# Conv1 outputs, phase differences and conv2 operands stored position by position, graphs innermost

## What is computed

```python
h = jnp.maximum(_layernorm(x, axis=-1), 0.0)            # (64, 128 nodes, 128)
xc = jnp.transpose(h, (0, 2, 1))
c = jax.nn.relu(_bn(_conv1d(xc, conv1_w, 0), ...))      # 1 tap
c = _bn(_conv1d(c, conv2_w, 8), ...)                    # 17 taps, padding 8
x_conv = jnp.transpose(jax.nn.relu(c + xc), (0, 2, 1))
A = jnp.exp(-dist(h @ w_se.T)) * adj                    # dist: squared distances
x_nmp = A @ jax.nn.relu(h @ w_msg.T + b_msg)
gi, gh = concat([x_conv, x_nmp]) @ w_ih.T + b_ih, h @ w_hh.T + b_hh
x = x + gru(gi, gh, h)                                  # gates r, z, n
x = x + adj @ (relu(layernorm(x)) @ weight) + bias      # second layer
```

## Time and profile before

| | |
|---|---|
| median of 3 runs | 414.94 us (414.62 to 416.28) |
| the profiled execution | 415.42 us, its span 413.2 us |
| PE busy | 352.8 us, 85% of the span |
| DVE, ACT, POOL busy | 289.6, 206.6, 175.7 us |
| mean granted TensorE clock | 0.924 of full speed |
| time from one conv1(a) to the next, steps 2 to 6 | 44.5 us each |

### The profile page before, as it was taken

One profiled execution on the slowest core, in us unless ns is written; L12 is line 12 of the kernel. 1 busy time (PEld: TensorE's weight loads), 2 busy tenths in 40 slices (PEclk: granted clock), 3 DMA queues, 4 the chain that ended last, 5 costly groups with the idle time before them and its releaser, 6 DMA issues.

```text
span 413.2 us, 6302 instructions
## 1 busy us (share of the span) xinstructions
PE 352.8 (85%) x2196; PEld 322.7 (78%) x2196; DVE 289.6 (70%) x736; ACT 206.6 (50%) x402; POOL 175.7 (43%) x140
## 2 busy tenths in 40 slices
PE   6465765997999799979999799979997999989935
PEld 6465755876898689869998799878986899889825
DVE  4768687757787679757875888767985787662471
ACT  2144841554634674475736573567437663442332
POOL 7524264020593039601872069203960197035021
PEclk9688888996999899998999899989999899999975
DMA  7500010000030003100210013000100000001001
GB/s 266 218 0 2 0 52 27 0 2 1 28 106 22 0 4 101 52 0 2 89 66 1 2 35 119 1 2 16 62 26 1 2 27 26 2 0 52 0 0 51
DMA packets 7806, 15.08 MB, mean 37 GB/s; under 512 B 992, under 2 KB 1376, under 8 KB 7648
## 3 DMA queue, kind: packets, MB, share of 16 engines
q1 hardware_dynamic: 7488, 14.56, 10.1%
q10 hardware_dynamic: 288, 0.14, 0.1%
HBM read 10.50 MB, written 4.19 MB: 36 GB/s over the span
## 4 chain that ended last, share of the span: by engine, by line
issue 43%; POOL 32%; DVE 11%; PE 7%; ACT 4%; DMA 1%; POOLq 0%; ACTq 0%; DVEq 0%
POOL work L1107 4%; POOL rs L1066 4%; POOL rs L1061 4%; POOL base L1117 3%; POOL base L1123 3%; POOL base L1119 3%; POOL px L769 3%; POOL px L759 3%; POOL ac L765 2%; POOL px L767 2%; POOL px L762 2%; DVE hn L802 2%; ACT hn L548 1%; DVE cx_lo L858 1%; PE pP L283 1%
## 5 line engine op out<-in xcount | busy, mean ns | idle before, releaser
L1066 POOL TENSOR_TENSOR rs<-ve,neg_half 128x4 f32<-128x4 f32 x16 | 16.1, 1008 | 150.5 <-DVE ve L899 150.5
L262 PE MATMUL pP<-cx_hi,conv_hi 128*128 128x256 f32 x176 | 55.6, 316 | 3.5 <-DVE conv_lo L863 3.5
L263 PE MATMUL pP<-cx_lo,conv_hi 128*128 128x256 f32 x176 | 52.6, 299 | 0.0
L264 PE MATMUL pP<-cx_hi,conv_lo 128*128 128x256 f32 x176 | 52.4, 298 | 0.0
L262 PE MATMUL pQ<-cx_hi,conv_hi 128*128 128x256 f32 x144 | 45.6, 317 | 3.0 <-DVE conv_lo L863 3.0
L263 PE MATMUL pQ<-cx_lo,conv_hi 128*128 128x256 f32 x144 | 43.0, 299 | 0.0
L264 PE MATMUL pQ<-cx_hi,conv_lo 128*128 128x256 f32 x144 | 43.0, 299 | 0.0
L262 PEld LDWEIGHTS pP<-cx_hi,conv_hi 128*128 128x128 f32 x176 | 35.4, 201 | 3.7 <-DVE conv_lo L863 3.7
L1061 POOL TENSOR_TENSOR rs<-ve,neg_half 128x8 f32<-128x8 f32 (+1 forms) x9 | 17.1, 1902 | 44.9 <-DVE ve L789 43.6
L263 PEld LDWEIGHTS pP<-cx_lo,conv_hi 128*128 128x128 f32 x176 | 35.2, 200 | 0.0
L264 PEld LDWEIGHTS pP<-cx_hi,conv_lo 128*128 128x128 f32 x176 | 35.0, 199 | 0.0
(11 more groups left out here) (233 smaller groups left out, 1044.3 us busy)
## 6 DMA issues: line engine op xcount, KB each, us to landing
x_ring<-x_in SPq DMA_DIRECT2D x16, 256.0 KB, 2.6
adj_ring<-adj_in SPq DMA_DIRECT2D x16, 256.0 KB, 3.4
out<-x_ring SPq DMA_DIRECT2D x16, 256.0 KB, 2.0
work<-conv_in SPq DMA_DIRECT2D x1, 1088.0 KB, 7.2
x_ring<-gate_in SPq DMA_DIRECT2D x1, 576.0 KB, 7.7
work<-bias_in SPq DMA_DIRECT2D x1, 132.0 KB, 7.1
early<-early_in SPq DMA_DIRECT2D x1, 129.5 KB, 3.0
late<-late_in ACTq DMA_DIRECT2D x1, 128.0 KB, 3.2
```

What stands on the lines that cost most here:

```text
L262: pe.matmul(acc, w_hi, m_hi, start=start, stop=False)
L263: pe.matmul(acc, w_hi, m_lo, start=False, stop=False)
L264: return pe.matmul(acc, w_lo, m_hi, start=False, stop=stop)
L1066: pool.tensor_tensor(rs2[g % 2][:], ve2[g % 2][:], neg_half[:, 0:GG], ALU.pow).then_inc(rs2_set, 1)
```

## The change

The axes "graph" and "position" are exchanged in `c1`, `ac`, `px`, `cx_hi`, `cx_lo` and `base`: a tile that was [phase, 8 graphs, 36 positions] is now [phase, 36 positions, 8 graphs]. The PSUM halves of conv2 and s22, s12, s32 have their columns in the same new order. `xc_hi` and `xc_lo` stay graph by graph, with the two phases of one e side by side within a graph (64 words), since the gates want graphs outermost. It follows for the accesses:

- The data operand of each of the 960 conv2 matmuls was eight runs of 32 words, 36 words apart, starting at word j; it is one run of 256 words, starting at word 8j.
- `conv1_out` on ACT wrote 16 runs of 32 words; it now writes 512 single words, 8 words (32 bytes) apart.
- `conv_round` on ACT read 512 adjacent words of `base`; it now reads single words 8 words apart, and writes adjacent ones. `conv_lo_out` on DVE does the same with one of its two inputs.
- `own` on POOL read hT in runs of 32 words; it now reads single words 128 words apart.
- `pre` 2 and 5 on POOL had 16 runs of 35 words, now two of 280. The other operations of POOL, `split_hi`, `split_lo`, `between` and `conv_out` cover the same adjacent words as before.
- `gates_c` read runs of 32 adjacent words, now of 64.

Each engine has the same instructions in the same order, with the same waits: 1620 rows on PE, 501 on DVE, 301 on ACT, 133 on POOL, 42 on SP. Lines of the changed kernel are 3 higher than before from `by_graph` to `conv_lo_out`, then 2 higher.

```diff
-        c1 = sb("c1", [128, PH, CG, QP])
-        ac = sb("ac", [128, 2, CG, QP])
-        px = sb("px", [128, 8, CG, QP])
-        cx_hi = sb("cx_hi", [128, 9, CG, QP], F32R)
-        cx_lo = sb("cx_lo", [128, 9, CG, QP], F32R)
+        c1 = sb("c1", [128, PH, QP, CG])
+        ac = sb("ac", [128, 2, QP, CG])
+        px = sb("px", [128, 8, QP, CG])
+        cx_hi = sb("cx_hi", [128, 9, QP, CG], F32R)
+        cx_lo = sb("cx_lo", [128, 9, QP, CG], F32R)
...
-        base = [sb(f"base{i}", [128, 2, CG, QN]) for i in range(2)]
-        xc_hi = sb("xc_hi", [128, PH, CG, QN], F32R)
-        xc_lo = sb("xc_lo", [128, PH, CG, QN], F32R)
+        base = [sb(f"base{i}", [128, 2, QN, CG]) for i in range(2)]
+        xc_hi = sb("xc_hi", [128, 2, CG, 2 * QN], F32R)
+        xc_lo = sb("xc_lo", [128, 2, CG, 2 * QN], F32R)
...
+        def by_graph(e):
+            return base[e][:].rearrange("p s m g -> p g (s m)")
...
-                                         cx_hi[:, x, :, j:j + QN], cx_lo[:, x, :, j:j + QN],
+                                         cx_hi[:, x, j:j + QN, :], cx_lo[:, x, j:j + QN, :],
...
-                act.activation(c1[:, :, j, 2:2 + QN].rearrange("p k g m -> p g k m"),
+                act.activation(c1[:, :, 2:2 + QN, j].rearrange("p k m g -> p g k m"),
...
-                act.activation(xc_hi[:, 2 * e:2 * e + 2], base[e][:], ACT.Relu).then_inc(xchi_set, 1)
+                act.activation(xc_hi[:, e], by_graph(e), ACT.Relu).then_inc(xchi_set, 1)
...
-                last = eng.tensor_tensor(px[:, X32:X23 + 1, :, 0:QP - 1], c1[:, 0:3:2, :, 1:QP],
-                                         c1[:, 3:4, :, 0:QP - 1].to_broadcast([128, 2, CG, QP - 1]), ALU.subtract)
+                last = eng.tensor_tensor(px[:, X32:X23 + 1, 0:QP - 1], c1[:, 0:3:2, 1:QP],
+                                         c1[:, 3:4, 0:QP - 1].to_broadcast([128, 2, QP - 1, CG]), ALU.subtract)
...
-                dve.scalar_tensor_tensor(xc_lo[:, 2 * e:2 * e + 2], base[e][:], 0.0,
-                                         xc_hi[:, 2 * e:2 * e + 2].bitcast(F32), ALU.max, ALU.subtract)\
+                dve.scalar_tensor_tensor(xc_lo[:, e], by_graph(e), 0.0, xc_hi[:, e].bitcast(F32), ALU.max, ALU.subtract)\
...
-                phases = hT[t % 2][:].rearrange("p (g k m) -> p k g m", g=CG, k=PH)
+                phases = hT[t % 2][:].rearrange("p (g k m) -> p k m g", g=CG, k=PH)
```

More of the change, by code:

```diff
@@ L380, in gates_c @@
                 j = slice(g % 2 * GG, (g % 2 + 1) * GG)
-                m_hi = xc_hi[:, :, j].rearrange("p k g m -> p g k m")
-                m_lo = xc_lo[:, :, j].rearrange("p k g m -> p g k m")
+                m_hi = xc_hi[:, :, j].rearrange("p e g n -> p g e n")
+                m_lo = xc_lo[:, :, j].rearrange("p e g n -> p g e n")
                 gate_part(pR, 0, 0, m_hi, m_lo, False, True).then_inc(r_done, 1)
@@ L758, in pre @@
             if k == 1:
-                last = eng.tensor_tensor(px[:, X12:X21 + 1], c1[:, 1:3], c1[:, 3:4].to_broadcast([128, 2, CG, QP]),
+                last = eng.tensor_tensor(px[:, X12:X21 + 1], c1[:, 1:3], c1[:, 3:4].to_broadcast([128, 2, QP, CG]),
                                          ALU.subtract)
             elif k == 2:
-                last = eng.tensor_tensor(px[:, X32:X23 + 1, :, 0:QP - 1], c1[:, 0:3:2, :, 1:QP],
-                                         c1[:, 3:4, :, 0:QP - 1].to_broadcast([128, 2, CG, QP - 1]), ALU.subtract)
+                last = eng.tensor_tensor(px[:, X32:X23 + 1, 0:QP - 1], c1[:, 0:3:2, 1:QP],
+                                         c1[:, 3:4, 0:QP - 1].to_broadcast([128, 2, QP - 1, CG]), ALU.subtract)
             elif k == 3:
-                last = eng.tensor_tensor(ac[:], c1[:, 0:2], c1[:, 2:3].to_broadcast([128, 2, CG, QP]), ALU.subtract)
+                last = eng.tensor_tensor(ac[:], c1[:, 0:2], c1[:, 2:3].to_broadcast([128, 2, QP, CG]), ALU.subtract)
             elif k == 4:
@@ L768, in pre @@
             else:
-                last = eng.tensor_tensor(px[:, X13:X33 + 1, :, 0:QP - 1], ac[:, :, :, 1:QP],
-                                         px[:, X12:X32 + 1:2, :, 0:QP - 1], ALU.subtract)
+                last = eng.tensor_tensor(px[:, X13:X33 + 1, 0:QP - 1], ac[:, :, 1:QP],
+                                         px[:, X12:X32 + 1:2, 0:QP - 1], ALU.subtract)
             last.then_inc(pre_set, 1)
@@ L913, in conv_out @@
                 have(dve, (sumE_set, sumO_set)[e], t + 1)
-                dve.scalar_tensor_tensor(base[e][:], (pQ, pP)[e][:].rearrange("p (s g m) -> p s g m", s=2, g=CG),
+                dve.scalar_tensor_tensor(base[e][:], (pQ, pP)[e][:].rearrange("p (s m g) -> p s m g", s=2, g=CG),
                                          bn_a[:, 1:2], base[e][:], ALU.mult, ALU.add).then_inc(ct_set, 1)
@@ L926, in between @@
                 have(dve, xclo_set, 2 * t)
-                dve.scalar_tensor_tensor(base[1][:].rearrange("p s g m -> p s (g m)"),
+                dve.scalar_tensor_tensor(base[1][:].rearrange("p s m g -> p s (m g)"),
                                          pQ[:].rearrange("p (s w) -> p s w", s=2), bn_a[:, 1:2],
@@ L1049, in _ @@
             pool.memset(ones_r[:].bitcast(F32), 1.0).then_inc(rows_zero, 1)
-            pool.memset(px[:, X32:X23 + 1, :, QP - 1:QP], 0.0)
-            pool.memset(px[:, X13:X33 + 1, :, QP - 1:QP], 0.0)
+            pool.memset(px[:, X32:X23 + 1, QP - 1:QP], 0.0)
+            pool.memset(px[:, X13:X33 + 1, QP - 1:QP], 0.0)
             pool.memset(pair[:, 0, :, :, 1, S:S + 1], 1.0)
@@ L1118, in sums @@
                 pool.wait_ge(sum_half, 3 * t + 1)
-                pool.tensor_tensor(base[0][:].rearrange("p s g m -> p s (g m)"),
-                                   base[0][:].rearrange("p s g m -> p s (g m)"),
+                pool.tensor_tensor(base[0][:].rearrange("p s m g -> p s (m g)"),
+                                   base[0][:].rearrange("p s m g -> p s (m g)"),
                                    s12[:].unsqueeze(1).to_broadcast([128, 2, CG * QN]), ALU.add)\
@@ L1125, in sums @@
                 pool.wait_ge(s32_set, t + 1)
-                pool.tensor_tensor(base[1][:].rearrange("p s g m -> p s (g m)"),
-                                   base[1][:].rearrange("p s g m -> p s (g m)"),
+                pool.tensor_tensor(base[1][:].rearrange("p s m g -> p s (m g)"),
+                                   base[1][:].rearrange("p s m g -> p s (m g)"),
                                    s32[:].unsqueeze(1).to_broadcast([128, 2, CG * QN]), ALU.add)\
```

## The result

| | before | after |
|---|---|---|
| median of the runs | 415.1 us (4 runs, 414.62 to 416.28) | 432.06 us (4 runs, 431.69 to 433.63) |
| profiled execution | 415.42 us | 431.69 us |
| its span | 413.2 us | 428.5 us |
| mean granted clock of TensorE | 0.924 | 0.918 |

The change makes the kernel slower: the ratio of the times is 1.0412, 95% interval 1.0378 to 1.0445. The forecast was 427.2 us in a range of 410 to 442. The direction and the place were right; the terms of the sum were not, and two of them were wrong in opposite directions.

What follows compares the result with a forecast made beforehand. No engine was full: PE bounds one stretch of a step, an ACT and DVE chain the other. Opening 1.2 + chains 6.9 + clock 5.0 - PE at the end 1.3 + last step 0.5 = +12.3: 427.2 us, range 410 to 442.

Steps and rivals of the forecast that it cites:

- The bound: Each step: PE's rate bounds conv1(a) to neighbour_sums(b); then ACT and DVE work sets when the next conv1(a) starts.
- the chain: End of each step, conv_out, rounding and conv_lo_out twice over ACT and DVE: 1.7 us longer, six steps net 6.9 us.
- Taps: conv2 matmuls on PE: aligned starts bring nine per product from 130 to 119 ns, 0.55 us per step on the path.
- what is saved in the first stretch is kept: From conv1(a) to neighbour_sums(b), the stretch bound by PE: its saving of 0.55 us per step counts in full.
- Single words: conv1_out, conv_round, conv_lo_out: 1.6 ns per single word, so 0.39 us more per ACT operation, 0.30 us on DVE.
- gates_c: PE waits up to 0.5 us for xc_lo before gates_c, inside the chain's time except in the last full step.
- The clock: Behind a wait before conv1(a) grown to 3.6 us, low granted clock costs steps 2 to 6 1.0 us each: 5.0 us.
- Opening and end: Opening: three conv1_out on the path, +1.2 us. End: PE saves 1.3 us, last full step's gates_c wait adds 0.5.
- (1): Rival: single words cost nothing on ACT and DVE, only PE's gain of 4.9 us is left, 410.0 us; chance 0.18.
- (2): Rival: only one of ACT and DVE pays, or both but the clock stays: 415 to 423 us; chance 0.18.
- (3): Rival: a single word costs 2.5 ns, the chain is 3.5 us longer, 442 us; chance 0.27.
- (4): Rival: PE's 130 ns per matmul are not due to where runs start, 432 us; chance 0.05.

Runs made afterwards that it cites:

- a_none: The changed kernel with all single-word accesses of conv1_out, conv_round, conv_lo_out and POOL's hT reads left out (values in wrong places): 412.52 us, ratio 0.9934.
- none_clock: a_none with twelve added 128-column matmuls ahead of conv1(a) in each step: 404.54 us, ratio 0.9746.
- b_clock: The kernel before with nine added 128-column matmuls, results unread, ahead of conv1(a) in each step: 406.06 us, ratio 0.9797.
- a_clock: The changed kernel with twelve added 128-column matmuls ahead of conv1(a) in each step: 420.44 us, ratio 1.0142.
- a_noown: The changed kernel with only POOL's reads of hT back in runs of 32 words (values added in wrong places): 423.47 us, ratio 1.0208.
- a_nowrite: The changed kernel with conv1_out on ACT writing runs of 32 adjacent words again, to wrong positions: 428.85 us, ratio 1.0312.
- a_oldtaps: The changed kernel with conv2's matmuls reading the same tiles in the old pattern of eight runs of 32 words (wrong operands): 434.31 us, ratio 1.0438.

## Why the prediction was right, and where it was wrong

**The bound, and the direction.** Right. The waits of PE named the chain behind conv2, the added time stands in it, and 11.7 of the 15.3 us are in steps that end with it. Most of the cause is shown by the kernels that take one part back: the reads of base alone are worth 13 us.

**Taps.** Right in size: 118 ns per matmul, 119 forecast. conv_out comes 0.40 to 0.66 us earlier in a step (0.55 forecast). Wrong in the sentence "what is saved in the first stretch is kept". It took the chain to begin when PE is ready, and left out POOL: conv_lo_out(e=0) does not end before POOL's line 767 has, and POOL's list is not shortened by faster taps. The 0.28 us that POOL took in the kernel before was read as an addition to the chain; it was the sign that POOL's list was already the later of the two. a_none and none_clock show it: 0.2 and 0 us are kept per step. The error is worth 6 x 0.35 to 0.55, 2 to 3 us.

**Single words.** The mechanism was right, the price too low: 1.6 ns per word was forecast, 1.8 (DVE read), 1.9 (ACT write) and 2.0 (ACT read) were measured. The price of a line on PE was too low by 0.2 to 0.4 ns, and since the pace of adjacent words (0.83 and 1.01 ns) is taken off, the measured additions are 30 to 54% above the forecast ones: 0.60, 0.54 and 0.39 us for 0.39, 0.39 and 0.30. The Trainium skill, "Vector Engine (DVE) Microarchitecture Reference", section 5.2, has about 1.7 ns for a stream that hops far; DVE's 1.8 is near it. (It is this figure, not the 1.05 ns for adjacent words, that the prediction means by "its first figure" near 1.6.) Its 2.5 ns is for steps of 24 words on both inputs or on the output; the one input at eight words' distance here does not show it.

**The chain.** Forecast 1.7 us longer per step, measured 2.5. It can be worked out without the clock, from the step of b_clock and a_clock that starts at 140.44 and 146.81: POOL's second-last difference ends 25.40 us after conv1(a) in the one and 26.05 in the other (+0.65: its two reads of hT, and DVE in its way); conv_lo_out(e=0) ends 0.54 and 0.97 us behind it (+0.43); the second rounding is 0.62 longer, the second conv_lo_out 0.39. The sum is 2.09 us, the measured difference of the steps. The first rounding, 0.60 us longer, is not in it: it is hidden behind POOL (in the kernel after it is done at 173.45, POOL's line 770 at 174.40). So the forecast's list (2 x ACT, 2 x DVE, 0.3 for POOL, less PE's 0.55) counted two things that POOL covers, one in each direction, and had 0.3 us for POOL where 0.65 was measured. How the 0.65 divides between the reads of hT and DVE in its way is shown in part: with the reads back in runs the chain is 0.49 us shorter (a_noown).

**gates_c.** 1.26 us of waiting in each step, 0.5 forecast; inside the chain's time, as said. The wait before conv1(a) is 3.18, 3.6 forecast, because that one and the 0.25 us before x_turn(a) take more of it than was forecast.

**The clock.** Too high: +5.0 us forecast, nothing in the five steps of the two records, and 2.6 us by the medians of the four kernels with and without the added matmuls, which is not clear of their noise. The step that failed was to read step 1 of the kernel before (3.06 us of waiting, a long low stretch) against steps 2 to 6 (2.35 us, a short one) as a price that grows with the wait. All waits of the kernel after are 3.18 us, longer than the one of step 1, and with them comes no low stretch, a short or a long one. A short one costs 1.3 to 1.5 us and a long one 2.4 to 2.6, from the steps of 45.1, 46.4 and 47.6 us and from 43.03 us in b_clock against 44.5 and 45.47 in the kernel before. Against the same five steps of b_clock and a_clock that is 8.4 us before and 7.7 after. The price was nearly right: a long stretch costs 1.0 to 1.2 us more than a short one. What did not come are long stretches in all of the five steps.

**Opening and end.** 1.2 us were forecast for conv1_out in the opening; 2.33 are its share, by a_nowrite. Three of four operations were counted at 0.39 us; four at 0.54 would be 2.2, which fits, but no run shows that the third one counts. The end is -0.25 us where -0.8 was forecast; between b_clock and a_clock it is -0.79 (92.11 and 91.32 us behind the last wait).

**The sum, again.** 0.95 (arrival of x) + 2.9 (opening) + 2.05 + 9.7 (six chains) + 0 (clock) - 0.25 = 15.3 us. The forecast was 1.2 + 6.9 + 5.0 - 0.8 = 12.3 us. That the total was near is luck: a clock term that did not come in these records stood in for a chain term that was 4.8 us too small. The rivals: (1) the single words are not free; (2) both engines pay and the clock stays, but the six steps bring 2.05 + 9.7 and not 6.9 us; (3) the price of 2.5 ns is not there; (4) run starts are PE's 130 ns (a_oldtaps).

## What to carry to other kernels

A layout that gives TensorE aligned runs hands the transposition to somebody: count who reads or writes single words that are 16 bytes or more apart (here some 0.4 to 0.6 us per 512 words on ACT and DVE), and where that stands, since some 0.1 us saved per product on PE was paid with 2.5 us in a chain. An operation that is longer than its twin, as conv_lo_out(e=0) was by 0.28 us, can mark a second list that ends at about the same time; ask what that list does when the first gets shorter. And a wait of the matmul engine that "costs nothing" can still be worth filling: read the granted clock behind it.

## What the runs showed of the hardware beyond that

- A step at 16 bytes, and little growth with the distance beyond it: conv_round at 512 words takes 0.63 us from adjacent words, 0.66 from every second, 1.12 from every fourth, 1.23 from every eighth.
- A DVE operation on two tiles of SBUF that meets a POOL operation of the same kind ends a nearly fixed time after it: 0.54 to 0.57 us in the kernel before, in a_none, none_clock and b_clock, with its own work of 0.69 us; 0.94 to 0.98 us in the kernel after and in a_clock, where its work is 1.08.
- With a wait of 3.18 us before conv1(a) comes no, a short or a long stretch of granted clock at 0.50 (1.2 of 2.4 GHz), at a price of 0, 1.35 or 2.55 us, in one and the same execution; filling a wait of 2.35 us with matmuls of no use took the low stretches away and 9 us (2%) off the kernel. What decides among the three is not settled here.
